# A fused Perceiver layer: the second expert bias as a matmul, and additions taken off POOL

## The reference

```python
x = x + cross_attention(layernorm(x), ctx)   # 16 heads of 64, softmax over 257 keys
x = x + time_mix(layernorm(x))               # RWKV-like mixing over the 32 tokens
# expert layer: D_MODEL, D_FF, N_EXP = 128, 512, 8
xf = layernorm(x).reshape(-1, 128)           # 4096 tokens
expert_idx = argmax(xf @ Wr.T + br)          # one expert for each token
h = relu(einsum('td,efd->etf', xf, W1) + b1[:, None, :])
y = einsum('etf,edf->etd', h, W2) + b2[:, None, :]
x = x + y[expert_idx, arange(4096)]
```

## Time and profile before

| | us |
|---|---|
| median of 3 runs (lowest to highest) | 949.33 (947.11 to 950.98) |
| the profiled execution, and its span | 950.45, 948.7 |
| busy PE / PEld | 858.7 (91%) / 712.5 (75%) |
| busy DVE / ACT / POOL | 806.1 (85%) / 683.1 (72%) / 788.3 (83%) |
| scatter on POOL begins | 793.17 |
| first load of a tile issued | 847.84 |
| mean granted clock of PE | 0.954 |

### The profile page before, as it was taken

The page is one execution under the profiler, slowest core; times in us unless marked ns, Lnnn a source line. Parts: engine busy times, 40 slices in busy tenths (PEclk is TensorE's granted clock), DMA queues, the critical chain, the costliest instruction groups (busy, mean ns, idle before and its releaser), DMA issues.

```text
span 948.7 us, 28634 instructions
## 1 busy us (share of the span) xinstructions
PE 858.7 (91%) x8486; PEld 712.5 (75%) x8486; DVE 806.1 (85%) x2058; ACT 683.1 (72%) x1956; POOL 788.3 (83%) x1218
## 2 busy tenths in 40 slices
PE   7999999999999999999999999999999874429992
PEld 7777787887888888888888888888887663427882
DVE  5899879898989898989898989989898967657882
ACT  3877787777878787887877787877887662308881
POOL 5798898989898989998999989898989754654885
PEclk9999999999999999999999999999999985659997
DMA  9122222222211221222221222112120032111220
GB/s 251 26 60 73 61 61 61 61 61 61 60 59 59 59 59 59 75 62 75 64 78 59 59 59 59 59 59 59 59 60 28 1 122 105 43 51 49 73 64 13
DMA packets 56704, 60.90 MB, mean 64 GB/s; under 512 B 8750, under 2 KB 50609, under 8 KB 56640
## 3 DMA queue, kind: packets, MB, share of 16 engines
q1 hardware_dynamic: 54144, 55.84, 20.2%
q0 software_dynamic: 2496, 4.26, 1.4%
HBM read 37.65 MB, written 23.34 MB: 64 GB/s over the span
## 4 chain that ended last, share of the span: by engine, by line
PE 35%; POOL 32%; issue 14%; DVE 11%; ACT 4%; POOLq 1%; SPq 1%; DMA 0%; DVEq 0%; ACTq 0%
POOL Pn L1040 12%; PE bank L392 7%; PE bank L443 5%; PE bank L414 4%; PE bank L436 4%; POOL cT L1031 3%; PE bank L404 3%; PE bank L420 3%; POOL out_dram L1430 3%; POOL chi L1021 2%; POOL e12p L1047 2%; DVE Tl L885 2%; POOL clo L1025 2%; POOL e12p L1050 1%; POOL yb L1424 1%
## 5 line engine op out<-in xcount | busy, mean ns | idle before, releaser
L813 ACT ACTIVATE Pe<-bank,nmax 128x257 f32<-128x257 f32 x512 | 241.5, 472 | 108.2 <-DVE nmax L881 89.2
L1040 POOL TENSOR_TENSOR Pn<-Pe,rsum 128x1028 f32<-128x1028 f32 x128 | 243.1, 1900 | 36.3 <-DVE rsum L905 28.8
L392 PE MATMUL bank<-cT,qh 96*128 96x257 f16 x1024 | 184.3, 274 | 5.7 <-ACT Pe L813 4.1
L885 DVE TENSOR_TENSOR Tl<-bank,Th 128x1024 f16<-128x1024 f32 x128 | 155.4, 1214 | 2.3 <-ACT Th L802 1.9
L443 PE MATMUL bank<-identf,Pn 128*128 128x128 f32 x1024 | 152.7, 275 | 0.6 <-POOL Pn L1040 0.4
L802 ACT ACTIVATE Th<-bank 128x512 f16<-128x512 f32 x256 | 141.0, 593 | 9.1 <-PE bank L443 9.0
L392 PE MATMUL bank<-cT,ql 96*128 96x257 f16 x512 | 139.1, 272 | 0.0
L392 PEld LDWEIGHTS bank<-cT,qh 96*128 96x128 f16 x1024 | 97.6, 97 | 44.9 <-issue 9.6
L443 PEld LDWEIGHTS bank<-identf,Pn 128*128 128x128 f32 x1024 | 114.2, 141 | 9.1 <-POOL Pn L1040 2.1
L881 DVE TENSOR_REDUCE nmax<-bank 128x2 f32<-128x514 f32 x128 | 88.1, 688 | 21.0 <-PE bank L392 19.9
L894 DVE TENSOR_REDUCE nmax<-bank 128x1 f32<-128x257 f32 x256 | 105.0, 412 | 0.0
(11 more groups left out here) (229 smaller groups left out, 2431.3 us busy)
## 6 DMA issues: line engine op xcount, KB each, us to landing
sorted_rows<-fill SPq DMA_DIRECT2D x30, 589.5 KB, 3.8
rawT<-in_dram SPq DMA_DIRECT2D x32, 385.5 KB, 4.5
raw<-in_dram SPq DMA_DIRECT2D x32, 384.0 KB, 5.1
xs<-sorted_rows SPq DMA_DIRECT2D x23, 131.0 KB, 2.2
R<-in_dram SPq DMA_DIRECT2D x4, 512.0 KB, 5.8
Z<-last_rows SPq DMA_DIRECT2D x128, 2.2 KB
w1r<-in_dram SPq DMA_DIRECT2D x4, 512.0 KB, 8.0
w2fr<-in_dram SPq DMA_DIRECT2D x4, 512.0 KB, 9.2
```

The costliest lines, as they stand in the source:

```text
L392: last = nc.tensor.matmul(bank[SB[t]][:, 0:M], w[:, par, b, t * P:(t + 1) * P], cT[:, s4, c, 0:M], start=(k == 0), stop=(k == 2))
L813: nc.scalar.activation(Pe[:, n_par(j + 1), t, :], bank[SB[t]][:, 0:M], ACT.Exp, bias=nmax[:, n_par(j + 1), t:t + 1], accum_out=sums[:, n_p ...
L885: nc.vector.tensor_tensor(Tl[:, n_par(j - 1), :, :], psum[:, 4:4 + MC, :], Th[:, n_par(j - 1), :, :], ALU.subtract).then_inc(s_Tl, 1)
L1040: nc.gpsimd.tensor_tensor(Pn[:, par, :, :], Pe[:, par, :, :], rsum[:, par, :].unsqueeze(2).broadcast_to([P, QT, M]), ALU.mult)\
```

## The change

b2 no longer goes through POOL and DVE. A table b2p holds, for each expert, the f16 high half of its bias in partition 0, the low half (b2 less its f16 value) in partition 1, and zeros in the other 126. PE multiplies a matrix of ones (onesh, which is there already) with the table's row block of the expert, at the start of each second layer, into the same banks; that is the sum of the two halves in every output row. The residual is then added from xs itself, and idx is read from xs too. As xs now lives until yout is made, it has XN = 8 buffers of 256 rows instead of 4; yb and b2b are gone. On POOL the loop keeps the two stores only, and they are those of tile s - 2 in step s (they were those of s - 3), behind a wait for yout of the same tile. The table is made on POOL in `pool_route_tables`, step n = 5 of the attention loop, by a memset and four operations over 1024 columns; SP loads b2 for it into two partitions, behind the loads of the router's weights, and no longer loads b2b at 772.8 us.

```diff
+    XN = 2 * UN
@@ names
+        b2r = asb("b2r", [2, E, C])
+        b2h = asb("b2h", [2, E, C], F16)
+        b2l = asb("b2l", [2, E, C])
+        b2p = asb("b2p", [P, E, C], F16)
-        b2b = lsb("b2b", [P, E, C + 1])
-        xs = lsb("xs", [P, UN, SUB, RW])
+        xs = lsb("xs", [P, XN, SUB, RW])
-        yb = lsb("yb", [P, UN, SUB, C + 1])
@@ pool_route_tables
+            wait(nc.gpsimd, s_b2, 16)
+            nc.gpsimd.memset(b2p[:, :, :], 0.0).then_inc(s_b2p, 1)
+            nc.gpsimd.tensor_copy(b2h[:, :, :], b2r[:, :, :]).then_inc(s_b2p, 1)
+            wait(nc.gpsimd, s_b2p, 2)
+            nc.gpsimd.tensor_tensor(b2l[:, :, :], b2r[:, :, :], b2h[:, :, :], ALU.subtract).then_inc(s_b2p, 1)
+            wait(nc.gpsimd, s_b2p, 3)
+            nc.gpsimd.tensor_copy(b2p[0:2, :, :], b2l[:, :, :]).then_inc(s_b2p, 1)
+            wait(nc.gpsimd, s_b2p, 4)
+            nc.gpsimd.tensor_copy(b2p[0:1, :, :], b2h[0:1, :, :]).then_inc(s_b2p, 1)
             nc.gpsimd.iota(R[:, :, C], pattern=[[P, G]], base=0, channel_multiplier=1,
@@ SP
+            sp.dma_start(b2r[:, :, :], b2.rearrange("(o e) d -> o e d", o=1).broadcast_to([2, E, C])).then_inc(s_b2, 16)
...
-            sp.dma_start(b2b[:, :, 0:C], b2.rearrange("(o e) d -> o e d", o=1).broadcast_to([P, E, C])).then_inc(s_w3, 16)
...
-                u = s % UN
-                wait(sp, s_t["xn"], s - UN + 1)
-                wait(sp, s_t["yb"], s - UN + 1)
+                u = s % XN
+                wait(sp, s_t["xn"], s - XN + 1)
+                wait(sp, s_t["out"], s - XN + 1)
@@ pool_tile
-                if exists(s - 3, NT):
-                    wait(pool, s_t["out"], s - 2)
-                if exists(s + 1, NT):
-                    w = (u + 1) % UN
-                    e = expert(u + 1)
-                    wait(pool, s_xs[w], 16 * (it + 1 + (u + 1) // UN))
-                    pool.wait_ge(s_w3, 16)
-                    nc.gpsimd.tensor_tensor(yb[:, w, :, :], xs[:, w, :, 0:C + 1],
-                                            b2b[:, bass.ds(e, 1), :].broadcast_to([P, SUB, C + 1]), ALU.add)\
-                        .then_inc(s_t["yb"], 1)
-                if exists(s - 3, NT):
-                    v = (u - 3) % UN
+                if exists(s - 2, NT):
+                    v = (u - 2) % UN
+                    wait(pool, s_t["out"], s - 1)
                     for m in range(SUB):
@@ pe_tile
+                    wait(pe, s_b2p, 5)
+                    for m in range(SUB):
+                        nc.tensor.matmul(bank[6 + m][:, 0:C], onesh[:, :],
+                                         b2p[:, bass.ds(e, 1), :].rearrange("p o c -> p (o c)"), start=True, stop=False)
...
-                                                        start=(f == 0 and k == 0), stop=(f == FC - 1 and k == 2))
+                                                        start=False, stop=(f == FC - 1 and k == 2))
@@ dve_tile
-                    w = (u - 2) % UN
-                    wait(dve, s_t["yb"], s - 1)
+                    w, x = (u - 2) % UN, (s - 2) % XN
+                    wait(dve, s_xs[x], 16 * ((s - 2) // XN + 1))
                     wait(dve, s_store[w], 16 * SUB * (it + (u - 2) // UN))
-                    nc.vector.tensor_copy(idx[:, w, :], yb[:, w, :, C])
+                    nc.vector.tensor_copy(idx[:, w, :], xs[:, x, :, C])
                     wait(dve, s_t["y"], s - 1)
-                    nc.vector.tensor_tensor(yout[:, w, :, :], psum[:, 6:6 + SUB, 0:C], yb[:, w, :, 0:C], ALU.add)\
+                    nc.vector.tensor_tensor(yout[:, w, :, :], psum[:, 6:6 + SUB, 0:C], xs[:, x, :, 0:C], ALU.add)\
                         .then_inc(s_t["out"], 1)
```

More of the change, by code:

```diff
@@ L247, in perceiver_layer_kernel @@
         s_f = {n: sem("f_" + n) for n in ("xn", "xT", "xc", "lg", "rt")}
-        s_xs = [sem(f"s_xs{u}") for u in range(4)]
+        s_xs = [sem(f"s_xs{u}") for u in range(XN)]
+        s_b2 = sem("s_b2")
+        s_b2p = sem("s_b2p")
         s_store = [sem(f"s_store{u}") for u in range(4)]
-        s_t = {n: sem("t_" + n) for n in ("xn", "xT", "xh", "xl", "h", "hr", "hh", "hl", "y", "yb", "out")}
+        s_t = {n: sem("t_" + n) for n in ("xn", "xT", "xh", "xl", "h", "hr", "hh", "hl", "y", "out")}
         block = top.enter_context(nc.Block())
@@ L1396, in _ @@
             pool.wait_ge(s_res, GB * G)
-            nc.gpsimd.memset(b2b[:, :, C:C + 1], 0.0).then_inc(s_ftab, 1)
             nc.gpsimd.iota(kk[:, :, :], pattern=[[CAP * TR, E], [TR, CAP]], base=0, channel_multiplier=0,
@@ L1432, in pool_tile @@
                             .then_inc(s_store[v], 16)
-            over_tiles(pool, pool_tile)
+            over_tiles(pool, pool_tile, routed=False)
         @block.scalar
@@ L1612, in _ @@
             dve_hot(0, GA)
-            dve.wait_ge(s_ftab, 12)
+            dve.wait_ge(s_ftab, 11)
             dve_rank(0, GA, 0)
@@ L1677, in dve_tile @@
                 if exists(s - 2, NT):
-                    w = (u - 2) % UN
-                    wait(dve, s_t["yb"], s - 1)
+                    w, x = (u - 2) % UN, (s - 2) % XN
+                    wait(dve, s_xs[x], 16 * ((s - 2) // XN + 1))
                     wait(dve, s_store[w], 16 * SUB * (it + (u - 2) // UN))
-                    nc.vector.tensor_copy(idx[:, w, :], yb[:, w, :, C])
+                    nc.vector.tensor_copy(idx[:, w, :], xs[:, x, :, C])
                     wait(dve, s_t["y"], s - 1)
-                    nc.vector.tensor_tensor(yout[:, w, :, :], psum[:, 6:6 + SUB, 0:C], yb[:, w, :, 0:C], ALU.add)\
+                    nc.vector.tensor_tensor(yout[:, w, :, :], psum[:, 6:6 + SUB, 0:C], xs[:, x, :, 0:C], ALU.add)\
                         .then_inc(s_t["out"], 1)
                 if exists(s + 3, NT):
-                    v, w = (u + 1) % 2, (u + 3) % UN
-                    wait(dve, s_xs[w], 16 * (it + 1 + (u + 3) // UN))
+                    v, w = (u + 1) % 2, (s + 3) % XN
+                    wait(dve, s_xs[w], 16 * ((s + 3) // XN + 1))
                     wait(dve, s_t["xT"], s + 2)
```

## The result

The changed kernel took 951.75 us (median of 20 runs, 949.62 to 955.30), the kernel before 949.41 on the same chip (20 runs, 947.11 to 951.80): ratio 1.0023, 95% interval 1.0014 to 1.0031. That is 2.3 us slower, inside the 0.5% that I had called no change, but on the other side of zero than the forecast of 1.5 us less. The time lies inside the stated 942 to 955 and 0.75 us above the 945 to 951 that I gave to the forecast's own case.

The account below looks back on a forecast made before the run. PE was taken to bound the attention stage, POOL's pace or a little below the expert loop, POOL alone the end. 6.1 - 2.6 - 5.0 = -1.5 us on the median of 949.33 gave 947.8 us, range 942 to 955.

Parts of the forecast that it names:

- the forecast's own case: Whole kernel: no measurable change, 947.8 us, with its bounds 945 to 951; chance 0.58.
- Part 1, the table: Attention stage, n = 5: five POOL operations take 6.4 us and cost +6.1 us (5.3 to 9.2).
- the 0.3 us that I took off as slack: Attention stage: all but about 0.3 of the table's 6.4 us reaches PE and DVE.
- the first rival: Table at n = 5 is cheap (943.7 us) or hidden (941.7 us), so the kernel is faster; chance 0.22.
- Part 2, the loop: Expert loop: period falls from 3.25 to 3.10 us over 17 periods, -2.6 us (nothing to -3.4).
- the even period of 3.10: Expert loop: each tile takes 3.10 us, from (6.09 + 0.11) / 2.
- the bias pair: Expert loop: PE's two added matmuls per tile take 0.11 us and lie in the two-tile ring once.
- the second store: Expert loop: POOL's second store of a tile runs from 3.21 to 4.18 us after yout starts; the idx copy misses it.
- the ring: Expert loop: a cycle through PE, ACT and DVE spanning two tiles, 6.09 us before the change, 3.05 each.
- POOL's pace: Expert loop before the change: POOL repeats every 3.21 us without waiting; the loop goes at that or a little below, 3.25.
- The second rival: Expert loop: stores collide with the idx copy, period 3.51 us, +4.4 instead of -2.6, total 955.3 us; chance 0.17.
- Part 3, the tail: Kernel end: last store ends 17.7 us after tile 20's start instead of 22.66, gain 5.0 us (4.5 to 5.8).

Follow-up runs that it names:

- no_bias: packs_early without the two bias matmuls of each tile (b2 left out of the output); ratio 0.9920 to the kernel before.
- half_stores: packs_early without the second output store of each tile, so half of the output rows are not written; ratio 0.9877 to the kernel before.
- packs_early: late_table with all three packs of expert numbers loaded at the expert loop's start, not at tiles 0, 8 and 16; ratio 0.9943 to the kernel before.
- late_table: The changed kernel with the table's load and POOL operations moved from n = 5 to near 780 us; 948.90 us, ratio 0.9964 to the kernel before.

## Why the prediction was right and wrong

**Part 1, the table: right.** 6.1 forecast, 6.3 measured. The rows behind it were right one by one: memset 0.95 (0.89), copies 1.03 (1.05), subtraction 2.12 (2.1). The waits on its own semaphore, for which I had no row, took 0.06 to 0.09 (0.08). Two partitions cost what the rows of 128 had led me to take, so the first rival is out; the Trainium skill's page GPSIMD Engine Reference (section 1), by which one core owns 16 partitions, is in line with that. Only the 0.3 us that I took off as slack was not there.

**Part 2, the loop: this step failed in size.** I forecast 52.7 us from tile 3 to tile 20, a gain of 2.6; PE shows 55.0, a gain of 0.3. What I drew of the first store was right (start 0.79 behind yout for 0.86, end 0.84 behind hl, idx copy free), but not the even period of 3.10: the periods alternate. Three terms were wrong, and each has its experiment:

- I counted the bias pair once in two tiles, 0.9 us in 17 periods. It costs 1.6 (no_bias).
- I put the second store at nothing, since the idx copy misses it; it costs 1.0 us (half_stores), and idx and xsn are what it stretches. I had read the ring from early periods, with xsn at 0.59, though the same trace had 0.72 to 0.74 in the later ones.
- I read 3.25 a tile as POOL's pace, though two of the 17 periods were long through loads of expert numbers, which stay: 0.6 us (packs_early).

The ring of the earlier trace rows without all these, 17 x 6.09 / 2 = 51.8, and 1.6 + 1.0 + 0.6 on top are 55.0, as measured. Against the forecast the loop lost 0.7 + 1.0 + 0.6 = 2.3 us; that the three simply add is arithmetic, not an experiment. So a loop that was bound by POOL near 3.2 a tile met a ring that the change itself had lengthened to nearly as much. The second rival (stores that collide with idx and hold the period at 3.51) did not come about: the idx copies are free. Its kin did, in xsn. The Trainium skill's page SBUF — State Buffer ("Who interferes with whom") infers that a tensor_tensor does not stall descriptor generation; the first stores of the first 18 tiles disagree, held to between 1.38 and 1.76 us in place of 0.98.

**Part 3, the tail: right in kind, 0.9 too large.** 5.0 forecast, 4.06 measured. The last yout came 0.35 later than forecast and the store backlog was 0.55 longer: from 916.7 us to the end POOL was never idle for more than 0.34 us, with stores held to 1.63, 1.15, 1.74 and 1.16 in between.

**The sum.** 6.3 - 0.3 - 4.1 = +1.9 instead of -1.5. Of the 3.4 us between the two, 2.3 are the loop's, 0.9 the tail's and 0.2 the table's. I had also carried the 1.75 us beyond the span over unchanged. It was 2.10 in the profiled execution of the changed kernel and 2.5 in the median of its 20 runs (2.09 on the other chip). Every kernel with the change has some 0.3 us more than the kernel before there, but for half_stores (1.78), so it seems to go with the stores; yet the kernel before ends in just such a row of stores 0.30 us apart, so a close row alone isn't it. This stays open, as do the single executions of up to 5.0 (late_table). With 0.35 the sum is +2.3. The medians part by 2.3 us on one chip; on the other by 1.2, or 1.4 (0.4 to 2.5) by the ratio.

## What to carry to other kernels

Work on an engine that has no idle is paid in full wherever it stands ahead of the first user, however few partitions it touches: move a table to a stage where that engine waits, and here 6.3 us come back by the timelines, some 5 to 5.6 by the ratios of late_table and the two comparisons of the changed kernel. Before a gain is claimed for lifting one limit, work out the next one with the change's own additions in it, period by period and not by the mean: periods that alternate, or that stand out at every eighth tile, belong to something else than the average suggests. And of two orders that both take work out of the same ring, the one that released PE's bank ahead of the long hl gained 3 to 4 us, and the one that released it behind hl lost 12.

## What the hardware showed that I had not expected

- GpSimd took 1.03 us for a cast of 1024 elements on two partitions and for a copy on one, and 2.12 for a subtraction on two, in line with 128-partition rows.
- An indirect store that started inside VectorE's tensor_tensor of two SBUF inputs and took 1.1 us or more ended 0.83 to 0.87 us behind it in all 13 traces. When it started 0.3, 0.7 and 0.9 us after its start, the store of 0.98 us took 1.75, 1.38 and 1.19.
- The reverse exists too: a GpSimd addition of 0.7 us that runs beside a tensor_scalar pair stretched it from 0.59 to 1.04, and stores that began 0.2 to 0.45 ahead of it to between 0.65 and 0.83; those that began 0.1 to 0.3 us after it left it at 0.59 to 0.65.
- What follows the last store is not a constant: to the end of the span 6.69 us in the kernel before and 4.84 in half_stores, and from there to the end of the run 1.71 to 1.80 in the kernel before and 2.04 to 3.56 in the two sets of runs of the changed kernel. No run here says why.
